# Attention and routed experts on one core: packed attention output, two banks for small products, scores by query in quarters of 64 queries, ranks in bf16

## The chip, the cores and the metric

The kernel runs as one launch on one core of a Trainium2 chip. The metric is the device time of the execution in microseconds (us). TensorE (PE) multiplies, VectorE (DVE), ScalarE (ACT) and GpSimd (POOL) do the elementwise work, SyncE (SP) issues most DMAs.

## The reference

```python
x = x + _layernorm(_L0_attn_ref(_layernorm(x), WQ, WK, WV, WO))   # 16 batches x 256 tokens x 128
x = x + _layernorm(_L0_ffn_ref(_layernorm(x), ...))
# attention: 16 heads of 8, causal softmax(Q K^T / sqrt(8)) V, then WO
# ffn: aff = x @ centroids.T; expert = argmax (8 experts); for each token its expert's
#      layernorm, w1 (128 -> 512), relu, w2 (512 -> 128), mixed with x by sigmoid(aff)
```

## The kernel before

**Tiling.** The 16 batches go through a software pipeline, one batch per step, 20 steps in all. In step i, batch i+3 is normalised and projected to Q and K, batch i+1 gets its scores by query, batch i its scores by key, exp and the product with V, and batches i-1 to i-4 the output projection, the layernorms, the choice of expert, the rank within it, and the scatter to rows sorted by expert in HBM. Afterwards 39 tiles of 128 sorted rows run through their experts.

**Q and K in three parts.** Q and K are split into three bf16 parts each (`project_qk`, `high`, `residue`, `middle`, `low`: PE, ACT, DVE, ACT, POOL). SP writes the parts to HBM (`parts_out`, L291) and reads them back in six DMAs (`parts_in`, L302 and L304) into `qaug` and `kaug`, 126 partitions deep, so that one bf16 product of depth 126 holds six products of parts.

**Scores twice.** `scores_by_query` (L802 to L812) puts queries on PSUM partitions so that DVE can take each row's maximum (`maxima`, L1082). The negated maximum, as two bf16 parts, is transposed by PE (`transpose_shift`, L787), copied by ACT (`shift_out`, L566) to `nmT`, and moved by a DMA of 8 KB (`shift`, L314, `aug<-nmT`) into the last two partitions of `qaug`: 16 source rows of each part become one long row. There are two such halves per batch, heads 0 to 7 and 8 to 15. `scores_near` and `scores_far` (L825, L834) then compute the shifted scores with keys on partitions, ACT takes exp, POOL applies the causal mask (L421, L425), and `weigh_values` (L846, L850) multiplies by V. V has 32 columns per head (8 values, a one, zeros), so four heads fill the 128 partitions of one output.

**What sets the order.** Each engine runs a stream written out by hand in its `step(i)`; semaphores join them. SP's is short: `shift(i, 1)`, `parts_out(i+2)`, `parts_in(i+2)`, `shift(i+1, 0)`, then in some steps one expert's w2. SP issues a DMA only when it has passed the waits and issues of all those ahead of it. PE's step starts with `scores_near(i, 0)`, which waits for the semaphore `sh_in[0]`, that is, until the DMA of `shift(i, 0)` has landed, and ends with `project_qk(i+3)` and one unit of scores by query.

**Scores by query before.** The work comes in 12 units of 512 columns per batch, which alternate between the two banks of `S`: 4 heads with queries 0 to 127 against keys 0 to 127, or 2 heads with queries 128 to 255 against all keys. Each begins with a product that writes the causal mask (L802, L807), and four products of 128 columns are added to it.

**Small products.** All the small products and transposes of a step (projections, transposes of x, of the output, of the maxima, the affinities and ranks) share one bank `M`. `take_m` makes PE wait before each until the one before has been read out.

Of the kernel before, what the change touches and what calls it, by code (L numbers as in the profile page):

```python
# [15 lines left out]
P = 128  # L16
# [35 lines left out]
def sandwich_kernel(nc, x, attn_w, w1x, w2t, b2, cent_t, out):  # L52
# [16 lines left out]
    CAP = (NT + 1) * P  # L69
    assert D == P and SEQ == 2 * P and B % 2 == 0  # L70

    RING = 3
# [8 lines left out]
    with ExitStack() as ctx:  # L81
# [17 lines left out]
        causal = sb("causal", [P, 4, P], BF16)  # L99
        before = sb("before", [P, P])  # L100
        ones = sb("ones", [P, P])
        mhalf = sb("mhalf", [P, NT])
# [19 lines left out]
        nmf = sb("nmf", [P, RING, NH, 2])  # L122
# [5 lines left out]
        oT = sb("oT", [P, 4, SEQ])  # L128
        rden = sb("rden", [P, 2, NH])
# [25 lines left out]
        hot = sb("hot", [P, NT, E])  # L155
        run = sb("run", [P, NT + 1, E])
# [16 lines left out]
        def carve(table, *shapes):  # L173
# [4 lines left out]
            for shape in shapes:  # L178
# [4 lines left out]
                if len(shape) == 3:  # L183
# [17 lines left out]
        O = ps("O", [P, 2, 2, SEQ])  # L201
        M = ps("M", [P, 512])

        names = ("w_attn w_cent w_ffn x_in x_next x_rest qzero kone ids_r consts pmem vmem vones "
                 "st_x agg_x ve_x rs_x nb_x xn_r xnT_r xnT_d qk_r hi_d r1_d mid_d parts_d "
# [26 lines left out]

        NA = FC // 2

        def hidden(p, c):

            if c < NA:
                return S[:, p, c * P:(c + 1) * P]
            return ST0[:, 2 * p:2 * p + 2].rearrange("p a n -> p (a n)")[:, (c - NA) * P:(c - NA + 1) * P]

# [37 lines left out]
        def _(sp):  # L278
# [110 lines left out]
        def _(pool):  # L389
# [53 lines left out]
            def scatter(b, t):  # L443

                p = b.slot(RING)
                if t == 0:
# [8 lines left out]
            g.memset(causal[:, :, :], 0.0).then_inc(s["pmem"], 1)  # L455
# [5 lines left out]
            g.affine_select(out=causal[:, :, :], in_=causal[:, :, :], compare_op=ALU.is_ge, fill=NEG, base=0,  # L461
                            pattern=[[0, 4], [-1, P]], channel_multiplier=1).then_inc(s["consts"], 1)
# [11 lines left out]
            for table, by, base in ((down, -1, E), (steps, P, 0), (slots, 1, 0), (starts, CAP, 0), (run[:, 0], CAP // P, 0)):  # L474
                g.iota(table[:, :], [[by, table.shape[-1]]], base=base, channel_multiplier=0,
                       allow_small_or_imprecise_dtypes=True).then_inc(s["consts"], 1)
            pool.wait_ge(s["ids_r"], 3)
# [60 lines left out]
        def _(act):  # L538
            a = nc.scalar

            def xnT_out(b):
# [4 lines left out]
                a.activation(xnT[:, p], M[:, 0:SEQ], ACT.Copy).then_inc(s["xnT_d"], 1)  # L546

            def high(b):
# [5 lines left out]
                a.activation(part(p, 0), M[:, :].rearrange("p (s t) -> p s t", s=2), ACT.Copy).then_inc(s["hi_d"], 1)  # L554
# [6 lines left out]
            def shift_out(b, half):  # L561
                act.wait_ge(s["shT_r"], b.times(2, half + 1))
                if b.follows(RING):
                    act.wait_ge(sh_in[half], b.times(16, 16 * (1 - RING)))
                p = b.slot(RING)
                a.activation(nmT[:, p, half], M[:, 0:P // 2].bitcast(BF16)[0:32, 0:P], ACT.Copy).then_inc(s["sh_d"], 1)  # L566

            def v_out(b):
# [20 lines left out]
            def o_out(i, half):  # L589
                act.wait_ge(s["pv"], i.times(NG, 2 * half + 2))  # L590
                if i.follows(1):
                    act.wait_ge(s["otr_r"], i.times(2))
                a.activation(oT[:, 2 * half:2 * half + 2], O[:, half], ACT.Copy).then_inc(s["o_ev"], 1)

            def onT_out(i):
# [3 lines left out]
                a.activation(onT[:, :], M[:, 0:SEQ], ACT.Copy).then_inc(s["onT_d"], 1)  # L599

            def y_out(i):
# [3 lines left out]
                a.activation(yb[:, i.slot(RING)], M[:, 0:SEQ].rearrange("p (t d) -> p t d", t=2), ACT.Copy).then_inc(s["y_d"], 1)  # L605

            def fT_out(i):
# [40 lines left out]
            def step(i):  # L648
# [5 lines left out]
                if t:  # L654
                    exp_far(t, 0)
                    shift_out(t, 1)
                if new:
                    normalise_x(new)
                if old:
                    o_out(old, 1)  # L660
# [17 lines left out]
                if t:  # L678
                    o_out(t, 0)
# [37 lines left out]
            def enter(t):  # L717
# [6 lines left out]
                a.activation(nT[:, p], (M, ST1[:, 0])[p][:, 0:P], ACT.Identity, scale=column(t, 0),  # L724
# [27 lines left out]
        def _(pe):  # L752
            mm = nc.tensor.matmul
            m_free = [[]]

            def take_m():
                for name, value in m_free[0]:
                    pe.wait_ge(s[name], value)

            def transpose_x(b):  # L760
                take_m()
                pe.wait_ge(s["xn_r"], b.times(1, 1))
                for t in (0, 1):
                    last = nc.tensor.transpose(M[:, t * P:(t + 1) * P], xn[:, b.slot(RING), t], ident[:, :])
# [3 lines left out]
            def project_qk(b):  # L768
                take_m()
                pe.wait_ge(s["xnT_d"], b.times(1, 1))  # L770
                for w in (0, 1):
                    last = mm(M[:, w * SEQ:(w + 1) * SEQ], wat[:, w], xnT[:, b.slot(RING)], start=True, stop=True)  # L772
                last.then_inc(s["qk_r"], 1)
                m_free[0] = [("hi_d", b.times(1, 1)), ("r1_d", b.times(1, 1))]

            def project_v(b):
                take_m()
# [725 lines left out]
```

## Time and profile before

| | |
|---|---|
| time, median of 3 runs | 454.77 us (454.33 to 455.31) |
| profiled execution, its own time | 454.81 us |
| its span, first to last instruction | 453.1 us |
| outside the span | 1.7 us |
| mean granted TensorE clock | 0.942 |
| PE busy | 359.6 us (79%) |
| DVE busy | 336.5 us (74%) |
| ACT busy | 250.8 us (55%) |
| POOL busy | 242.1 us (53%) |
| chain that ended last: PE, DMA, DVE, ACT | 54%, 11%, 9%, 4% |
| of it DMA `aug<-nmT` | 6% |

Busy time is the share of the span in which an engine had an instruction in flight. The chain is the sequence of work, each released by the one before, that ends with the last instruction. A row of the timeline gives start, length, engine, line, operation, output and inputs, count, and in brackets how long the engine had been idle and what ended it. The steps of the pipeline run to about 334 us, the experts' tiles after that.

### The profile page before, as it was taken

The page shows a single profiled execution, that of the slowest core. Times are in us where ns is not written, and L with a number is a line of the kernel's source. Part 1 is how long each engine was busy: PE and PEld are TensorE (multiplying, and loading weights), DVE is VectorE, ACT ScalarE, POOL GpSimd, SP SyncE. Part 2 cuts the span into 40 slices and gives each one's busy share as a digit, 9 for nine tenths or more (in the row PEclk, how much of TensorE's full clock was granted, in tenths as well). Part 3 has the DMA queues.
Part 4 walks back from the last instruction along what each step waited for, and adds up shares of the span by engine and source line. Part 5 has one row for each costly group of instructions (what it writes and reads, how often), then busy time and mean ns, then how long its engine had stood idle before and what let it go on. Part 6 is the DMA issues. An engine that isn't in the chain of part 4 may idle for free.

```text
span 453.1 us, 11940 instructions
## 1 busy us (share of the span) xinstructions
PE 359.6 (79%) x3739; PEld 286.3 (63%) x3739; DVE 336.5 (74%) x1244; ACT 250.8 (55%) x574; POOL 242.1 (53%) x334
## 2 busy tenths in 40 slices
PE   3359688979989998999899898987525798999960
PEld 1136466656767777777677766765424688888860
DVE  7748776758877887887887889575551788989880
ACT  2204457556675675675675665574203577777750
POOL 3803254534474664664664664567360266767773
PEclk9999989989999999999999999899555999999995
DMA  7661853726535535535526527021024466666720
GB/s 207 109 104 41 135 90 48 112 57 94 90 66 78 91 71 72 98 64 79 99 51 93 95 42 117 26 63 34 14 85 128 116 165 170 174 172 176 186 58 9
DMA packets 34686, 42.83 MB, mean 95 GB/s; under 512 B 5465, under 2 KB 25053, under 8 KB 33088
## 3 DMA queue, kind: packets, MB, share of 16 engines
q1 hardware_dynamic: 31744, 37.43, 42.3%
q0 software_dynamic: 2304, 4.37, 2.9%
q8 instruction: 31, 0.51, 0.6%
q14 instruction: 31, 0.25, 0.2%
q10 hardware_dynamic: 576, 0.27, 0.2%
HBM read 30.59 MB, written 11.66 MB: 93 GB/s over the span
## 4 chain that ended last, share of the span: by engine, by line
PE 54%; DMA 11%; DVE 9%; issue 9%; POOL 6%; SPq 5%; ACT 4%; POOLq 0%; DVEq 0%; ACTq 0%
PE O L846 6%; DMA aug<-nmT 6%; PE O L1006 5%; PE ST L825 5%; PE S L812 4%; PE S L993 4%; PE M L858 3%; PE M L772 3%; PE S L807 3%; PE S L805 3%; PE S L802 3%; PE O L850 3%; PE ST L993 2%; PE ST L834 2%; POOL out_x L516 2%
## 5 line engine op out<-in xcount | busy, mean ns | idle before, releaser
L1082 DVE TENSOR_REDUCE nmf<-S 128x2 f32<-128x512 f32 (+1 forms) x192 | 130.1, 680 | 53.7 <-PE S L812 26.7
L421 POOL TENSOR_SCALAR_AFFINE_SELECT p<-p 128x512 f32<-128x512 f32 x64 | 40.8, 638 | 96.9 <-ACT p L583 96.9
L583 ACT ACTIVATE p<-ST 128x1024 f32<-128x1024 f32 x64 | 65.5, 1023 | 16.6 <-PE ST L825 15.9
L812 PE MATMUL S<-aug 126*128 126x128 bf16 x512 | 51.7, 225 | 0.0
L825 PE MATMUL ST<-aug 128*128 128x256 bf16 x256 | 39.9, 279 | 14.9 <-DMA aug<-nmT 14.7
L425 POOL TENSOR_SCALAR_AFFINE_SELECT p<-p 128x512 f32<-128x512 f32 x64 | 40.9, 639 | 10.4 <-ACT p L587 7.8
L516 POOL DMA_INDIRECT out_x<-vaug,x_all x39 | 40.7, 1045 | 8.3 <-issue 6.1
L812 PEld LDWEIGHTS S<-aug 126*128 126x128 bf16 x512 | 41.2, 101 | 3.8
L526 POOL TENSOR_TENSOR rsz<-vez,mhalf 128x1 f32<-128x1 f32 x39 | 22.1, 567 | 39.0 <-DVE vez L1437 38.9
L1006 PE MATMUL O<-w_tab,vaug 128*128 x312 | 42.6, 280 | 0.0
L846 PE MATMUL O<-p,vaug 128*32 128x256 f32 x512 | 41.2, 391 | 0.3 <-POOL p L421 0.3
L451 POOL DMA_INDIRECT xs_rows<-pay,pos x32 | 32.9, 1029 | 13.1 <-DVE pos L1242 7.1
L587 ACT ACTIVATE p<-ST 128x512 f32<-128x512 f32 x64 | 38.7, 604 | 1.5 <-PE ST L834 0.3
L1006 PEld LDWEIGHTS O<-w_tab,vaug 128*128 128x128 f32 x312 | 37.8, 191 | 1.0 <-issue 0.2
L807 PE MATMUL S<-causal,identb 128*128 128x256 bf16 x128 | 36.5, 285 | 1.2 <-DVE nmf L1082 0.8
L825 PEld LDWEIGHTS ST<-aug 128*128 128x128 bf16 x256 | 23.4, 99 | 19.5 <-DMA aug<-nmT 17.1
L1408 DVE TENSOR_SCALAR vaug<-ST,w1s 128x128 f32<-128x128 f32 x78 | 23.7, 345 | 14.8 <-PE ST L993 12.8
L993 PE MATMUL S<-vaug,w1s 128*128 128x128 f32 x156 | 27.0, 297 | 7.3 <-DMA w1s<-in_w1x 3.4
L802 PE MATMUL S<-causal,identb 128*128 128x512 bf16 x64 | 26.0, 406 | 7.2 <-DMA aug<-qk_parts 7.2
L993 PEld LDWEIGHTS S<-vaug,w1s 128*128 128x128 f32 x156 | 21.2, 197 | 13.3 <-issue 6.8
L415 POOL TENSOR_TENSOR qkp<-res,qkp 128x512 bf16<-128x512 f32 x16 | 18.7, 1168 | 20.3 <-ACT qkp L559 20.3
L805 PEld LDWEIGHTS S<-aug 126*128 126x128 bf16 x256 | 21.1, 103 | 9.7 <-issue 2.2
(155 smaller groups left out, 868.4 us busy)
## 6 DMA issues: line engine op xcount, KB each, us to landing
w1s<-in_w1x SPq DMA_DIRECT2D x39, 259.0 KB
qk_parts<-qkp SPq DMA_DIRECT2D x16, 384.0 KB, 2.8
aug<-qk_parts SPq DMA_DIRECT2D x32, 192.0 KB
aug<-qk_parts SPq DMA_DIRECT2D x32, 128.0 KB
x_all<-xs_rows SPq DMA_DIRECT2D x39, 67.0 KB, 2.4
aug<-qk_parts SPq DMA_DIRECT2D x32, 64.0 KB
w_tab<-in_w2t SPq DMA_DIRECT2D x8, 256.0 KB, 5.6
out_x<-vaug,x_all POOLq DMA_INDIRECT x39
```

Source lines behind the costliest of these rows:

```text
L421: g.affine_select(out=v, in_=v, compare_op=ALU.is_ge, fill=0.0, base=0, pattern=[[0, 4], [1, P]], channel_multiplier=-1).then_inc(s["sel0" ...
L425: g.affine_select(out=v, in_=v, compare_op=ALU.is_ge, fill=0.0, base=0, pattern=[[0, 4], [1, P]], channel_multiplier=-1).then_inc(s["sel1" ...
L516: g.indirect_dma_start(out=out.rearrange("b t d -> (b t) d"), out_offset=bass.IndirectOffsetOnAxis(ap=xs[:, q, TOK:TOK + 1].bitcast(U32), ...
L583: a.activation(p0[:, gr % 2], ST0[:, :, :], ACT.Exp, scale=SCALE).then_inc(s["exp0"], 1)
L802: mm(bank, identb[:, :], causal[:, :, :], start=True, stop=False)
L807: mm(bank.rearrange("p (j c n) -> p j c n", j=2, c=2)[:, :, 1], identb[:, :], causal[:, 0:2], start=True, stop=False)
L812: last = mm(bank[:, j * SEQ + kb * P:j * SEQ + (kb + 1) * P], q[:, h, P:SEQ], k[:, h, kb * P:(kb + 1) * P], start=False, stop=(j == 1 and ...
L825: last = mm(ST0[:, j], kaug[:, p, h, 0:P], qaug[:, p, h], start=True, stop=True)
L846: mm(O[32 * j:32 * j + 32, gr // 2, gr % 2, :], vaug[:, p, 0, 4 * gr + j], p0[:, gr % 2, j], start=True, stop=False)
L993: last = mm(hidden(p, c), w1s[:, t.slot(WR), c * P:(c + 1) * P], nT[:, p], start=True, stop=True)
L1006: last = mm(O[:, p, 0, 0:D], hs[:, p, c], w2_tab[:, bass.ds(e * (FC * D) + c * D, D)], start=(c == 0), stop=(c == FC - 1))
L1082: v.tensor_reduce(dst, S[:, n % 2].rearrange("p (j n) -> p j n", j=k), op=ALU.max, axis=AX_X, negate=True).then_inc(s["red"], 1)
```

## The change

- `scores_by_query` works on quarters of 64 queries, with two heads (h and h+4) stacked on the 128 partitions, each product 64 columns wide in its weights. A quarter takes only the keys that it can see: 64, 128, 192 or 256. This makes 10 units of 512 columns per batch: in each half two of quarter 3, one of quarter 1 and two that join quarters 2 and 0. The causal mask, now 64 by 64 and doubled on the partitions, is added last.
- `maxima` takes one or two reduces per unit, 14 per batch. Since the maxima's rows now hold two heads of 64 queries, each `shift` becomes two DMAs of 4 KB.
- `weigh_values` puts the heads of an odd group 16 rows above those of the even group before it: the output takes one bank instead of two, leaves by one copy (`o_out`), four transposes and one `divide`. `v_out` takes two copies.
- The bank set free makes `M` two: `MA` and `MB`, with a list of waits each.
- The matrices of the ranks (`before`, `ones`, `hot`, `run`) are bf16, with values offset so that they are exact.
- On DVE `alphas` and `shift_parts` move by some places; on ACT `o_out` stands ahead of `normalise_x`.

```diff
+    QB = P // 2
+    UNITS = 10
-        oT = sb("oT", [P, 4, SEQ])
+        oT = sb("oT", [P, 2, SEQ])
-        O = ps("O", [P, 2, 2, SEQ])
-        M = ps("M", [P, 512])
+        O = ps("O", [P, 2, SEQ])
+        MA = ps("MA", [P, 512])
+        MB = ps("MB", [P, 512])
...
-                sp.dma_start(qaug[SHIFT:P, p, 8 * half:8 * half + 8].rearrange("c h (q t) -> c (h q) t", t=P),
-                             nmT[:, p, half]).then_inc(sh_in[half], 16)
+                for h in (0, 1):
+                    at = 8 * half + 4 * h
+                    sp.dma_start(qaug[SHIFT:P, p, at:at + 4].rearrange("c h (j t) -> c (h j) t", t=QB),
+                                 nmT[:, p, half, QB * h:QB * h + QB]).then_inc(sh_in[half], 16)
...
                 bank = S[:, n % 2]
                 q, k = qaug[0:SHIFT, p], kaug[0:SHIFT, p]
+                def score(pair, quarter, col):
+                    keys = QB * (quarter + 1)
+                    for h in (0, 1):
+                        head = 8 * half + 4 * h + pair
+                        mm(bank[QB * h:QB * h + QB, col:col + keys], q[:, head, QB * quarter:QB * quarter + QB],
+                           k[:, head, 0:keys], start=(col == 0), stop=False)
+                if kind < 2:
+                    for r in (0, 1):
+                        score(2 * kind + r, 3, 2 * P * r)
...
+                mm(masked, identb[:, :], causal[:, 0:blocks], start=False, stop=True).then_inc(s["s_r"], 1)
...
                 for j in range(4):
-                    mm(O[32 * j:32 * j + 32, gr // 2, gr % 2, :], vaug[:, p, 0, 4 * gr + j], p0[:, gr % 2, j],
-                       start=True, stop=False)
+                    mm(O[32 * j:32 * j + 32, gr // 2, :], vaug[:, p, 0, 4 * gr + j], p0[:, odd, j],
+                       start=not odd, stop=False)
...
-            def transpose_o(i, qb):
-                take_m()
-                pe.wait_ge(s["o_ev"], i.times(2, 2))
-                for gr in range(NG):
-                    last = nc.tensor.transpose(M[:, gr * P:(gr + 1) * P], oT[:, gr, qb * P:(qb + 1) * P], ident[:, :])
+            def transpose_o(i):
+                take_m(1)
+                pe.wait_ge(s["o_ev"], i.times(1, 1))
+                for qb in (0, 1):
+                    for half in (0, 1):
+                        at = 2 * qb + half
+                        last = nc.tensor.transpose(MB[:, at * P:(at + 1) * P], oT[:, half, qb * P:(qb + 1) * P], ident[:, :])
```

SP's stream in a middle step, from the second half's shift of one batch to the first half's of the next. Before:

```order
L314 DMA aug<-nmT 2x16x128 [waits st1_r,sh_d]
L291 DMA qk_parts<-qkp 128x6x256 [waits aug_in0,parts_d]
L302 DMA aug<-qk_parts 24x4096 [waits st1_r,qk_w0]
L304 DMA aug<-qk_parts 24x4096
L302 DMA aug<-qk_parts 16x4096
L304 DMA aug<-qk_parts 16x4096
L302 DMA aug<-qk_parts 8x4096
L304 DMA aug<-qk_parts 8x4096
```

The same place now:

```order
L337 DMA aug<-nmT 2x16x64 [waits st1_r,sh_d]
L337 DMA aug<-nmT 2x16x64
L312 DMA qk_parts<-qkp 128x6x256 [waits aug_in0,parts_d]
L323 DMA aug<-qk_parts 24x4096 [waits st1_r,qk_w0]
L325 DMA aug<-qk_parts 24x4096
L323 DMA aug<-qk_parts 16x4096
L325 DMA aug<-qk_parts 16x4096
L323 DMA aug<-qk_parts 8x4096
L325 DMA aug<-qk_parts 8x4096
L337 DMA aug<-nmT 2x16x64 [waits st1_r,sh_d]
L337 DMA aug<-nmT 2x16x64
```

A second DMA of the shift stands ahead of `parts_out` (L312), and another at the end.

PE's stream at the end of a step and the start of the next, where `sh_in0` is waited for. Before:

```order
L846 MATMUL O<-p,vaug 32x256 [waits sel0,o_ev]
L846 MATMUL O<-p,vaug 32x256 x3
L850 MATMUL O<-p,vaug 32x128 [waits sel1]
L850 MATMUL O<-p,vaug 32x128 x3
L772 MATMUL M<-xnT,wat 128x256 [waits xnT_d,onT_d]
L772 MATMUL M<-xnT,wat 128x256
L807 MATMUL S<-causal,identb 128x2x128 [waits red]
L812 MATMUL S<-aug 128x128 x4
L825 MATMUL ST<-aug 128x256 [waits exp0,sh_in0]
L825 MATMUL ST<-aug 128x256 x3
```

Now:

```order
L798 MATMUL MB<-xnT,wat 128x256 [waits xnT_d,v_d]
L798 MATMUL MB<-xnT,wat 128x256
L862 MATMUL ST<-aug 128x256 [waits exp0,sh_in0]
L862 MATMUL ST<-aug 128x256 x3
L835 MATMUL S<-aug 64x256 [waits red,aug_in2]
L835 MATMUL S<-aug 64x256 x3
L851 MATMUL S<-causal,identb 128x2x64
L914 MATMUL MA<-wo,onT 128x128 [waits onT_d]
L914 MATMUL MA<-wo,onT 128x128
L871 MATMUL ST<-aug 128x128 [waits exp1]
L871 MATMUL ST<-aug 128x128 x3
```

The unit between the projection (L772, now L798) and `scores_near` (L825, now L862) is gone; each unit is products of 64 weight columns with the mask behind them.

## Rows read from the trace of the kernel before

**Rows 1.** Timeline of PE at the start of three later steps and two early ones.

```profile
163.82 0.61 PE L825 MATMUL ST<-aug 128*128 128x256 bf16 x4 [1.00 <-DMA aug<-nmT]
...
180.88 0.61 PE L825 MATMUL ST<-aug 128*128 128x256 bf16 x4 [0.82 <-DMA aug<-nmT]
...
111.28 0.61 PE L825 MATMUL ST<-aug 128*128 128x256 bf16 x4 [0.71 <-DMA aug<-nmT]
129.39 0.61 PE L825 MATMUL ST<-aug 128*128 128x256 bf16 x4 [1.58 <-DMA aug<-nmT]
```

**Rows 2.** Timeline of SP's DMA issues over two steps.

```profile
149.39 0.62 SPq L314 DMA_DIRECT2D aug<-nmT  x1
150.11 0.39 SPq L291 DMA_DIRECT2D qk_parts<-qkp  x1
153.43 0.30 SPq L302 DMA_DIRECT2D aug<-qk_parts  x1
158.24 9.02 SPq L314 DMA_DIRECT2D aug<-nmT  x2
167.35 0.39 SPq L291 DMA_DIRECT2D qk_parts<-qkp  x1
170.13 0.30 SPq L302 DMA_DIRECT2D aug<-qk_parts  x1
184.59 0.39 SPq L291 DMA_DIRECT2D qk_parts<-qkp  x1
```

**Rows 3.** DMA view, 161 to 164 us: GB/s in 40 slices.

```profile
GB/s 219 0 0 0 109 0 0 0 0 0 0 3 7 3 7 7 7 7 7 10 7 3 7 7 7 10 7 3 0 0 0 0 0 0 0 0 0 0 0 0
```

**Rows 4.** DMA view, 149 to 151.5 us: busy tenths, GB/s.

```profile
DMA  0099500000000000000000009011110027999989
GB/s 0 0 480 412 206 0 0 0 0 0 0 0 0 0 0 0 0 0 0 0 0 0 0 0 262 0 25 29 41 25 12 0 49 205 303 262 311 287 254 270
```

**Rows 5.** Timeline of ACT at the start of a step.

```profile
164.18 0.63 ACT L559 ACTIVATE qkp<-res 128x512 bf16<-128x512 f32 x1 [0.97 <-DVE res L1070]
164.72 1.01 ACT L583 ACTIVATE p<-ST 128x1024 f32<-128x1024 f32 x1
165.62 0.38 ACT L605 ACTIVATE yb<-M 128x256 f32<-128x256 f32 x1
166.36 0.25 ACT L566 ACTIVATE nmT<-M 32x128 bf16<-32x128 bf16 x1
```

**Rows 6.** Timeline of POOL: the last part of Q and K.

```profile
165.97 1.18 POOL L415 TENSOR_TENSOR qkp<-res,qkp 128x512 bf16<-128x512 f32 x1
```

**Rows 7.** Waits, 60 to 300 us: who for whom, total, times, longest.

```profile
PE ST L825 <- DMA aug<-nmT: 11.6, 10, 3.1
...
PE M L764 <- DVE on L1109: 4.2, 12, 0.5
PE M L787 <- ACT yb L605: 3.8, 8, 0.6
```

**Rows 8.** Timeline of PE inside steps.

```profile
160.25 0.39 PE L812 MATMUL S<-aug 126*128 126x128 bf16 x4
160.57 0.64 PE L846 MATMUL O<-p,vaug 128*32 128x256 f32 x8
161.02 0.40 PE L850 MATMUL O<-p,vaug 128*32 128x128 f32 x8
...
168.12 0.39 PE L805 MATMUL S<-aug 126*128 126x128 bf16 x4
168.35 0.61 PE L858 MATMUL M<-ident,oT 128*128 128x128 f32 x4
168.79 0.39 PE L834 MATMUL ST<-aug 128*128 128x128 bf16 x4
```

**Rows 9.** Groups by line, whole span.

```profile
L1082 DVE TENSOR_REDUCE nmf<-S 128x2 f32<-128x512 f32 (+1 forms) x192 | 130.1, 680 | 53.7 <-PE S L812 26.7
L805 PEld LDWEIGHTS S<-aug 126*128 126x128 bf16 x256 | 21.1, 103 | 9.7 <-issue 2.2
```

More of the change, by code:

```diff
@@ L239, in hidden, with unit, units @@
             return ST0[:, 2 * p:2 * p + 2].rearrange("p a n -> p (a n)")[:, (c - NA) * P:(c - NA + 1) * P]
+        def unit(gr, u):
+            return 5 * (gr // 2) + 3 * (gr % 2) + u
+        def units(gr):
+            return 2 if gr % 2 else 3
         def iterations(eng, step):
@@ L473, in _ @@
             g.iota(fill_at[:, :], [[0, 1]], base=E * CAP, channel_multiplier=1).then_inc(s["ids_r"], 1)
-            for table, by, base in ((down, -1, E), (steps, P, 0), (slots, 1, 0), (starts, CAP, 0), (run[:, 0], CAP // P, 0)):
+            for table, by, base in ((down, -1, E), (steps, P, 0), (slots, 1, 0), (starts, CAP, -BASE), (run0, CAP // P, -P)):
                 g.iota(table[:, :], [[by, table.shape[-1]]], base=base, channel_multiplier=0,
                        allow_small_or_imprecise_dtypes=True).then_inc(s["consts"], 1)
+            pool.wait_ge(s["consts"], 11)
+            for table, by in ((run[:, 0], run0), (beforeb, before), (onesb, ones)):
+                g.tensor_copy(table[:, :], by[:, :]).then_inc(s["consts"], 1)
             pool.wait_ge(s["ids_r"], 3)
@@ L918, in _ @@
             pe.wait_ge(s["consts"], 6)
+            pe.wait_ge(s["mask_d"], 2)
             for gr in range(NG):
-                for u in range(3):
+                for u in range(units(gr)):
                     scores_by_query(Nth(0), gr, u)
@@ L970, in _ @@
             iterations(pe, step)
-            take_m()
-            mm(M[:, 0:E], ones[:, :], run[:, NT], start=True, stop=True).then_inc(s["total_r"], 1)
+            take_m(0)
+            mm(MA[:, 0:E], onesb[:, :], run[:, NT], start=True, stop=True).then_inc(s["total_r"], 1)
             pe.wait_ge(s["rt"], 1)
@@ L1078, in maxima @@
[L1078 to L1083 removed]
+                if u >= units(gr):
+                    return
+                p, n = b.slot(RING), unit(gr, u)
+                half, kind = n // 5, n % 5
@@ new lines, in maxima, with most @@
+                dve.wait_ge(s["s_r"], b.times(UNITS, n + 1))
+                def most(quarter, first, count, src):
+                    return v.tensor_reduce(nmf[:, p, half, first:first + count, quarter], src, op=ALU.max, axis=AX_X,
+                                           negate=True)
+                if kind == 2:
+                    last = most(1, 0, 4, S[:, n % 2].rearrange("p (r n) -> p r n", r=4))
+                else:
+                    two = S[:, n % 2].rearrange("p (r n) -> p r n", r=2)
+                    if kind < 2:
+                        last = most(3, 2 * kind, 2, two)
+                    else:
+                        most(2, 2 * (kind - 3), 2, two[:, :, 0:3 * QB])
+                        last = most(0, 2 * (kind - 3), 2, two[:, :, 3 * QB:4 * QB])
@@ L1085, in maxima_and_stats @@
+                last.then_inc(s["red"], 1)
             def maxima_and_stats(i, b, gr, u):
                 maxima(b, gr, u)
-                if i.k < 2:
-                    x_stats(i.k + 3, 3 * gr + u)
+                if i.k < 2 and u < units(gr):
+                    x_stats(i.k + 3, unit(gr, u))
             def shift_parts(b, half):
                 p = b.slot(RING)
-                src = nmf[:, p, 8 * half:8 * half + 8].rearrange("p h q -> p (h q)")
-                dve.wait_ge(s["red"], b.times(12, 6 * half + 6))
+                src = nmf[:, p, half].rearrange("p r j -> p (r j)")
@@ L1095, in shift_parts @@
+                dve.wait_ge(s["red"], b.times(UNITS, 5 * half + 5))
                 if b.follows(RING):
```

244 lines of the change are left out of this document (123 added, 121 removed).

## The prediction

> **What bounds the kernel now.** I read the table of the profile first: PE is busy 79% of the span and DVE 74%, so PE looks like the bound. Then I read the timeline of PE over a few steps for the places where it stands still. At the start of nearly every step it does: the first product of `scores_near` starts at 163.82 and 180.88 after 1.00 and 0.82 us of idling, both put down to the DMA `aug<-nmT` [rows 1]. Over 60 to 300 us PE lost 11.6 us there, more than to any bank [rows 7]. The next question is what makes this 8 KB late, so I read SP's issues. One step of it: shift issued at 149.39, taking 0.62; `parts_out` at 150.11; the first `parts_in` at 153.43; the next batch's first shift at 158.24; the next `parts_out` at 167.35 and then 184.59, so a step takes 17.24 us [rows 2]. The DMA view shows why the shift issued at 158.24 lands so late. In the idle queue of 149 to 151.5 us the small packets (5 slices of 0.0625 us at 12 to 41 GB/s) begin about 1.2 us after the issue at 149.39 and take 0.3 us [rows 2, 4]. The shift of 158.24 shows its small packets only from about 161.8 to 163.1, behind the last large ones of `parts_in` at 161.3 [rows 3]. So it waits in the queue for `parts_in`, and its own issue time is hidden.
>
> This closes a circle of one step: `scores_near` starts (163.82); ACT takes exp_near (164.72), the y copy (165.62), exp_far and `shift_out` (166.36) [rows 5]; SP issues `shift(i, 1)`, 0.62 us, which must have begun by 166.63 and ends just ahead of `parts_out` at 167.35 [rows 2]; `parts_in` follows 2.8 us later at 170.13, its data flows, the queued shift goes, and `scores_near` starts at 180.88. The other input of `parts_out`, the `low` part on POOL, ends at 165.97 + 1.18 = 167.15, so it is ready at about the same time [rows 6]. A second circle is almost as long: in ACT's stream exp_near at 164.72 follows `middle` (164.18), which waited for DVE's `residue` [rows 5]. `scores_near` has its four products issued by about 164.4, so the DMA circle has a slack of at most 0.3 us against the second one. I take 0.3: the DMA circle alone needs 16.95 us in later steps. In early ones, whose w2 loads share the queue, it has no slack: 129.39 - 111.28 = 18.1 us from one start to the next, with a wait of 1.58 [rows 1].
>
> **The change part by part.**
>
> *Shift as two DMAs.* The second half's shift stands ahead of `parts_out` on SP. Its second DMA has as many rows (2x16) of half the length, and I cost its issue like the first: 0.62 us plus 0.04 between two issues, 0.66 us on the circle. Bounds: 0.3, the shortest issue in SP's rows (`parts_in`), and 0.62 + 0.1 [rows 2]. In the first half's shift the second issue is hidden behind the data of `parts_in` (3.3 us of queue), but its packets are not: 8 KB took 0.3 us in an idle queue and 1.2 us behind `parts_in` [rows 3, 4]. With twice as many packets of half the size the addition is between 0 (both DMAs side by side) and 1.2; I take 0.45, nearest to the idle row. The sum for the circle is 16.95 + 0.66 + 0.45 = 18.06 us, or 0.83 more than 17.24 in a later step and 1.11 more in an early one.
>
> The DMA view shows one busy tenth while the shift's packets go [rows 4], that is, few of the 16 engines. By the Trainium skill, "DMA: Bandwidth & Descriptors", section "Why a DMA increments its semaphore by 16 and not by 1", a DMA uses the largest number of engines that divides the outermost dimensions of both sides, here 2 and 32, thus 2. By that rule the two DMAs, if they get the same two engines, queue behind one another, and the sum would lie above mine.
>
> *The two banks.* They free PE of the wait for y before the transposed shift (3.8 us in all) and of the wait for `on` before the transpose of x (4.2 us) [rows 7]. `residue` no longer stands behind a reduce, since the unit after `project_qk` is gone. All this shortens the second circle and PE's work between two DMA waits; on the first circle it shortens nothing, for ACT's chain from `scores_near` to `shift_out` remains: exp, y, exp, copy. What is late next is the same DMA, and PE waits for it longer. I cost these gains at nothing. If the DMA's cover were gone, they would be worth 0.3 + 0.35 us a step.
>
> *Scores by query on PE.* Before, a batch has 12 x 512 columns of products and 4096 of masks, 10,240 in all. Four products of 128 columns take 0.23 us [rows 8], so 10,240 columns, or 80 times 128, take 80 x 0.057 = 4.6 us. Now it is 10,240 columns of products and 2048 of masks. The four heads of `weigh_values` (eight passes of 256 columns in 161.02 - 160.57 = 0.45 us, where one after another at that rate they would take 0.9) show that products in different column groups run side by side. If the two stacked heads do so too, it is 5120 + 2048 columns = 3.2 us; if not, 5.5. To that come changes between narrow and full products. `L812` takes 0.32 us ahead of the narrow `L846` where `L805` takes 0.23 ahead of full ones [rows 8]: 0.09 each, 20 of them per step, 1.8 us. So PE's units go from 4.6 to 5.0 or 7.3 us.
>
> A rule speaks against the change here: the Trainium skill, "TensorEngine Tiling (Array Packing)", section "Tiling Modes", says that changing the tiling mode drains TensorE. The 0.09 us above is such a drain in this trace, and by it each of the ten units pays for two. The same page's promise of up to twice the speed for 64 columns would save 2.3 us of 5.5 and lose 1.8 of it to the drains.
>
> *The other PE work.* Four transposes less, at 168.79 - 168.35 = 0.44 us for four [rows 8], and about 0.35 us less for the ranks as one bf16 pass each: -0.8 us. PE's work per step, now 17.24 less waits of about 1.6, or 15.6, becomes 15.2 (15.6 + 5.0 - 4.6 - 0.8) or 17.5 (with 7.3). Both fit under 18.06, so its net cost is nothing. Above, if no weight load of the 64 is hidden at 0.10 us each [rows 9], units cost 6.4 + 1.8 + 0.9 = 9.1 us and PE's work 19.3.
>
> *DVE, ACT, POOL.* A reduce of 512 columns takes 0.68 us; 12 become 14 over 5120 columns instead of 6144 [rows 9], so DVE saves between 0.4 and 1.0 us a step, plus one pair of division. It idled before nearly each reduce, waiting for PE, so this is hidden. ACT saves one output copy and gains one V copy, off the circle.
>
> *Start and end.* The first batch's units run alone, ten instead of twelve, at half clock: -0.7 us, from 0 to -1.5. The last steps have no `parts_in`; they are chains of small products, and one set of four transposes, its division and two rank passes go from some of them: -1.7 us, from 0 to -2.5. The expert tiles are unchanged.
>
> *The sum.* `parts_out` inside a step occurs 14 times (of 16; two are at the start). The 5 early starts cost 1.11 each, the 9 later ones 0.83: 5.6 + 7.5 = 13.0. One early `parts_out` was held by `low` and not by the shift: -0.6. 13.0 - 0.6 - 2.4 = +10.0 us. The profiled execution took 454.81 us, 0.04 above the median of the runs, so the same sum holds for both: 464.8, say 465 us.
>
> **Rivals.**
>
> *The DMA's additions are small or hidden, and the banks pay (faster).* If the second issue overlaps the first, and its packets go beside the others, the DMA circle stays at 16.95 us and the second circle, now shorter by the y copy and the reduce, no longer holds it: 9 x 0.3 + 2.4 = 5 us less, 450. If moreover the wait at `scores_near` is shorter than the trace has it (a shift that goes ahead of the last packets of `parts_in`), PE's 15.2 us plus rest waits of 0.8 decide: 14 x 1.2 + 2.4, or 19 us less, 436. For it: the banks' waits are real [rows 7], and the idle queue moves 8 KB in 0.3 us. Against it: the 0.62 us stand bare between shift and `parts_out` in each step. It decides once the two additions are under 0.3 us a step.
>
> *They cancel.* Additions of 0.3 to 0.5 us, as with the lower issue price: 14 x 0.2 - 2.4, about 0: 453.9 to 455.7.
>
> *PE takes over (slower still).* At 19.3 us a step the circle of DMA is covered: 14 x 2.06 - 2.4 = +26, 481 us. For it: 64 loads per step, and the drains. Against it: the narrow fp32 loads of `weigh_values` are hidden.
>
> **How the numbers follow.** Forecast (DMA circle longer): 0.62, with its own range 458 (additions of 0.66 a step without the packets) to 474 (0.66 + 0.9). Faster: 0.21. Cancel: 0.07. PE takes over: 0.10. A measurement of this kernel can tell 0.2%, 0.9 us, from no change. Slower 0.72, same 0.07, faster 0.21. The range for 8 in 10 reaches from 446 (most of the faster cases) to 474.
>
> **What would show it.** Right: SP's rows have two `aug<-nmT` issues of about 0.6 us ahead of `parts_out`, steps of about 18.1 us from one `parts_out` to the next, PE idle 1.5 to 3 us before `scores_near`, and no wait for `y` or `on` at the small products. PE busy per unit about 0.5 us. Wrong: steps under 17.2 us, or PE not idle before `scores_near`, or an issue well under 0.6 us.

## The result, and the profile after

| | before | changed |
|---|---|---|
| time, median of the runs side by side (4 each) | 454.55 us (452.79 to 455.31) | 466.17 us (465.51 to 467.83) |
| profiled execution, its own time | 454.81 us | 465.54 us |
| its span | 453.1 us | 463.6 us |
| mean granted TensorE clock | 0.942 | 0.914 |
| PE, DVE busy | 359.6, 336.5 us | 354.5, 312.9 us |
| chain that ended last: PE, DMA | 54%, 11% | 42%, 25% |

The changed kernel takes 1.0244 times as long (95% interval 1.0204 to 1.0284). The forecast was 465 us, slower, by a longer circle of DMA. Ratios and differences of kernels go by runs within 1.5% of the fastest of their kernel; a_warm, below, had three slower ones in ten, and its other seven have a median of 455.1 us. PE and DVE have less work than before, and the chain has moved from PE to the DMA `aug<-nmT`. The page of the changed kernel, its clock, its chain and three groups (busy, mean ns, idle time ahead and its releaser):

```profile
PEclk9999997989999899899999998799755999999995
...
PE 42%; DMA 25%; SPq 10%; issue 7%; DVE 7%; POOL 5%; ACT 2%; POOLq 0%; DVEq 0%; ACTq 0%
DMA aug<-nmT 19%; PE S L835 9%; PE O L883 5%; PE ST L862 5%; PE S L851 5%; DMA w1s<-in_w1x 3%; PE ST L871 2%; SPq L337 2%; PE O L887 2%; PE MA L914 2%; PE S L1031 2%; SPq L386 2%; SPq L390 2%; POOL out_x L542 2%; PE ST L1031 1%
...
L1126 DVE TENSOR_REDUCE nmf<-S 128x2 f32<-128x512 f32 (+3 forms) x224 | 113.5, 531 | 70.7 <-PE S L851 68.8
L835 PE MATMUL S<-aug 126*64 126x256 bf16 (+3 forms) x1024 | 71.5, 254 | 2.8 <-DMA aug<-qk_parts 1.6
L862 PE MATMUL ST<-aug 128*128 128x256 bf16 x256 | 39.5, 278 | 38.0 <-DMA aug<-nmT 38.0
```

Waits of 60 to 300 us; the columns are those of [rows 7]. There PE waited 11.6 us for the shift, and now 33.1. The waits for y and for `on` ahead of the small products are gone:

```profile
PE ST L862 <- DMA aug<-nmT: 33.1, 13, 4.1
```

SP's issues in three steps. Line 337 is the shift, 312 `parts_out`, 323 the first `parts_in` (314, 291 and 302 in [rows 2]); a row with x4 spans both halves' pairs and the time between them:

```profile
162.36 9.62 SPq L337 DMA_DIRECT2D aug<-nmT  x4
172.08 0.39 SPq L312 DMA_DIRECT2D qk_parts<-qkp  x1
174.84 0.30 SPq L323 DMA_DIRECT2D aug<-qk_parts  x1
...
189.32 1.26 SPq L337 DMA_DIRECT2D aug<-nmT  x2
190.69 0.39 SPq L312 DMA_DIRECT2D qk_parts<-qkp  x1
194.75 0.30 SPq L323 DMA_DIRECT2D aug<-qk_parts  x1
...
226.86 1.26 SPq L337 DMA_DIRECT2D aug<-nmT  x2
228.22 0.39 SPq L312 DMA_DIRECT2D qk_parts<-qkp  x1
230.99 0.31 SPq L323 DMA_DIRECT2D aug<-qk_parts  x1
```

The pair takes 1.26 us where one took 0.62 [rows 2]. From the start of `scores_near` to `parts_out` it is 228.22 - 224.03 = 4.19 us in the last of these steps, and was 167.35 - 163.82 = 3.53 [rows 1, 2]: 0.66 more. The starts of `scores_near` on PE (compare [rows 1]), and further rows of the same timeline, which answer to [rows 8]:

```profile
150.18 0.61 PE L862 MATMUL ST<-aug 128*128 128x256 bf16 x4 [2.14 <-DMA aug<-nmT]
167.87 0.61 PE L862 MATMUL ST<-aug 128*128 128x256 bf16 x4 [1.00 <-DMA aug<-nmT]
185.29 0.61 PE L862 MATMUL ST<-aug 128*128 128x256 bf16 x4 [2.16 <-DMA aug<-nmT]
205.59 0.61 PE L862 MATMUL ST<-aug 128*128 128x256 bf16 x4 [3.58 <-DMA aug<-nmT]
224.03 0.61 PE L862 MATMUL ST<-aug 128*128 128x256 bf16 x4 [1.71 <-DMA aug<-nmT]
224.57 0.41 PE L835 MATMUL S<-aug 126*64 126x256 bf16 x4
224.91 0.23 PE L851 MATMUL S<-causal,identb 128*128 128x128 bf16 x1
224.98 0.66 PE L914 MATMUL MA<-wo,onT 128*128 128x128 f32 x4
...
241.34 0.61 PE L862 MATMUL ST<-aug 128*128 128x256 bf16 x4 [2.05 <-DMA aug<-nmT]
...
277.32 0.61 PE L862 MATMUL ST<-aug 128*128 128x256 bf16 x4 [2.79 <-DMA aug<-nmT]
```

From 150.18 to 277.32 are seven steps, 18.16 us each; 18.06 was forecast for a later step. But they are not alike. Busy time and granted clock of an early step and of five of the seven, and then one microsecond at a time near the start of the longest:

```profile
core 0: us, PE busy (x) PEld busy (x) DVE busy (x) ACT busy (x) POOL busy (x), PEclk, DMA share, GB/s
74.13:93.04 18.91, 17.02 (x192) 10.65 (x193) 11.55 (x36) 10.62 (x20) 9.30 (x13) 0.84 0.47 79
167.87:185.29 17.42, 15.26 (x201) 10.09 (x201) 13.50 (x54) 11.55 (x25) 11.22 (x16) 1.00 0.47 80
185.29:205.59 20.30, 16.72 (x201) 10.92 (x201) 12.57 (x49) 11.39 (x24) 11.71 (x17) 0.92 0.42 71
205.59:224.03 18.44, 16.74 (x200) 10.98 (x201) 12.29 (x48) 11.07 (x24) 8.49 (x13) 0.91 0.42 70
224.03:241.34 17.31, 15.26 (x200) 10.10 (x201) 12.84 (x51) 11.58 (x25) 10.60 (x15) 1.00 0.47 79
241.34:259.27 17.93, 15.27 (x201) 10.10 (x201) 12.56 (x49) 11.26 (x24) 10.93 (x16) 1.00 0.45 76
...
186.00:187.00 1.00, 1.00 (x8) 0.69 (x5) 0.36 (x1) 0.96 (x1) 1.00 (x1) 0.50 0.21 69
187.00:188.00 1.00, 1.00 (x9) 0.74 (x10) 0.33 (x1) 0.38 (x1) 0.68 (x2) 0.50 0.00 0
188.00:189.00 1.00, 1.00 (x10) 0.46 (x14) 0.19 (x1) 0.60 (x1) 0.31 (x1) 0.50 0.00 0
189.00:190.00 1.00, 1.00 (x18) 0.58 (x10) 0.89 (x3) 0.29 (x2) 0.33 (x1) 0.81 0.00 0
```

The four of the seven at full clock take 17.31 to 18.05 us, 17.7 in the mean. In the other three PE is granted 0.50, which is 1.2 of 2.4 GHz, for some 3 us after it stood at the DMA (2.14 us ahead of 150.18, 2.16 ahead of 185.29, 3.58 ahead of 205.59), just when it has the products that ACT's chain to the shift needs; four early steps have 0.84 to 0.92 in the mean. At 241.34 it stood 2.05 us and at 259.27 it stood 2.66, and kept its clock, so the wait alone doesn't tell when the clock falls. Of the 13 steps from 55.30 to 296.27 the clock fell in 8. In the 5 others it is 4.19 to 4.21 us from `scores_near` to `parts_out`, in the 8 it is 4.28 to 5.91. In the step from 185.29, `parts_out` comes 190.69 - 185.29 = 5.40 us after `scores_near`, 1.2 more than at 224.03. The same step has its first `parts_in` 4.06 us after `parts_out` instead of 2.8, as the step from 93.04 has it 4.49 after. No run explains this, and it comes in other kernels too (4.0 to 4.5 us in two steps each of a_warm and b_split1).

### The profile page after: what moved, and what is told of

It reads as the page before. It is cut to its first block, busy times and chain, and to the rows that moved or that the text cites. A ratio compares the mean times of both kernels' runs of the same rounds, so it can differ in the third digit from the quotient of the medians.

```text
span 463.6 us, 12161 instructions
## 1 busy us (share of the span) xinstructions
PE 354.5 (76%) x3866; PEld 252.3 (54%) x3866; DVE 312.9 (68%) x1249; ACT 248.1 (54%) x574; POOL 244.8 (53%) x337
## 4 chain that ended last, share of the span: by engine, by line
PE 42%; DMA 25%; SPq 10%; issue 7%; DVE 7%; POOL 5%; ACT 2%; POOLq 0%; DVEq 0%; ACTq 0%
DMA aug<-nmT 19%; PE S L835 9%; PE O L883 5%; PE ST L862 5%; PE S L851 5%; DMA w1s<-in_w1x 3%; PE ST L871 2%; SPq L337 2%; PE O L887 2%; PE MA L914 2%; PE S L1031 2%; SPq L386 2%; SPq L390 2%; POOL out_x L542 2%; PE ST L1031 1%
## 5 line engine op out<-in xcount | busy, mean ns | idle before, releaser
L1126 DVE TENSOR_REDUCE nmf<-S 128x2 f32<-128x512 f32 (+3 forms) x224 | 113.5, 531 | 70.7 <-PE S L851 68.8
L444 POOL TENSOR_SCALAR_AFFINE_SELECT p<-p 128x512 f32<-128x512 f32 x64 | 40.8, 638 | 104.8 <-ACT p L611 104.8
L835 PE MATMUL S<-aug 126*64 126x256 bf16 (+3 forms) x1024 | 71.5, 254 | 2.8 <-DMA aug<-qk_parts 1.6
L862 PE MATMUL ST<-aug 128*128 128x256 bf16 x256 | 39.5, 278 | 38.0 <-DMA aug<-nmT 38.0
L835 PEld LDWEIGHTS S<-aug 126*64 126x64 bf16 x1024 | 35.1, 113 | 30.4 <-issue 21.7
L862 PEld LDWEIGHTS ST<-aug 128*128 128x128 bf16 x256 | 23.7, 99 | 46.8 <-DMA aug<-nmT 43.7
L448 POOL TENSOR_SCALAR_AFFINE_SELECT p<-p 128x512 f32<-128x512 f32 x64 | 42.2, 659 | 11.6 <-ACT p L615 8.3
L883 PE MATMUL O<-p,vaug 128*32 128x256 f32 x512 | 44.8, 420 | 0.7 <-POOL p L444 0.7
L851 PE MATMUL S<-causal,identb 128*128 128x256 bf16 (+1 forms) x160 | 43.5, 272 | 0.0
L474 POOL DMA_INDIRECT xs_rows<-pay,pos x32 | 33.1, 1034 | 13.2 <-DVE pos L1296 7.4
L1464 DVE TENSOR_SCALAR vaug<-ST,w1s 128x128 f32<-128x128 f32 x78 | 23.6, 344 | 14.9 <-PE ST L1031 13.5
L851 PEld LDWEIGHTS S<-causal,identb 128*128 128x128 bf16 x160 | 15.5, 97 | 25.2 <-issue 16.9
L887 PE MATMUL O<-p,vaug 128*32 128x128 f32 x512 | 27.2, 283 | 0.0
L871 PE MATMUL ST<-aug 128*128 128x128 bf16 x256 | 26.7, 231 | 0.0
L731 ACT ACTIVATE vaug<-x_all 128x128 f32<-128x128 f32 x39 | 19.3, 494 | 13.5 <-DMA x_all<-xs_rows 13.5
```

The lines of the kernel that those rows point to most:

```text
L444: g.affine_select(out=v, in_=v, compare_op=ALU.is_ge, fill=0.0, base=0, pattern=[[0, 4], [1, P]], channel_multiplier=-1).then_inc(s["sel0" ...
L448: g.affine_select(out=v, in_=v, compare_op=ALU.is_ge, fill=0.0, base=0, pattern=[[0, 4], [1, P]], channel_multiplier=-1).then_inc(s["sel1" ...
L835: mm(bank[QB * h:QB * h + QB, col:col + keys], q[:, head, QB * quarter:QB * quarter + QB], k[:, head, 0:keys], start=(col == 0), stop=False)
L851: mm(masked, identb[:, :], causal[:, 0:blocks], start=False, stop=True).then_inc(s["s_r"], 1)
L862: last = mm(ST0[:, j], kaug[:, p, h, 0:P], qaug[:, p, h], start=True, stop=True)
L883: mm(O[32 * j:32 * j + 32, gr // 2, :], vaug[:, p, 0, 4 * gr + j], p0[:, odd, j], start=not odd, stop=False)
```

## Experiments

Each ran in a group with the kernel before, whose medians were 454.85 us in the first group (the first four below), 454.43 in the second (the next four), and 454.96 in the third. The ratios are the recorded ones, taken against these runs; they are not quotients of the medians and differ from them by up to 0.4% (a_early has 0.9697, and 442.82 / 454.85 is 0.9736).

### The double shift alone, in the kernel before

**b_split1**: the second half's shift, ahead of `parts_out`, as two DMAs. **b_split0** the same for the first half only, **b_split01** for both.

```diff
-                sp.dma_start(qaug[SHIFT:P, p, 8 * half:8 * half + 8]..., nmT[:, p, half]).then_inc(sh_in[half], 16)
+                parts = 2 if half in (1,) else 1
+                n = P // parts
+                for k in range(parts):
+                    sp.dma_start(dst[:, :, n * k:n * k + n], nmT[:, p, half, n * k:n * k + n]).then_inc(sh_in[half], 16)
```

> The kernel before, with the second half's shift (the one ahead of parts_out on SP) sent as two DMAs of 4 KB; nothing else is changed. Theory (the DMA circle): 0.66 us more issue ahead of parts_out, less the slack of 0.3 us: +0.36 us in 9 later steps and +0.66 in 5 early ones, +6.5 us, about 461 us; steps of about 17.6 us from parts_out to parts_out. Rival (the loss of the changed kernel is PE's work on narrow products, not the DMA): no change, 454.6 us.

> The kernel before, with only the first half's shift (the one queued behind parts_in) sent as two DMAs of 4 KB. Theory: its issue is hidden behind the data of parts_in, its packets are not: +0.45 us, less the slack of 0.3: 9 x 0.15 + 5 x 0.45 = +3.6 us, about 458 us. If the packets go side by side: no change. Rival (PE's work is the loss): no change, 454.6 us.

> The kernel before, with both halves' shifts as two DMAs of 4 KB each, as the changed kernel has them, and none of its other parts. Theory: the whole loss is here and somewhat more, since the gains at the start and the end (2.4 us) are missing: 5 x 1.11 + 9 x 0.81 = +12.8, about 467.5 us. Rival (PE's work is the loss): 454.6 us. Mixed: in between.

Measured: 465.91 us (ratio 1.0246, interval 1.0193 to 1.0298), 457.24 (1.0035, 1.0011 to 1.0058) and 467.12 (1.0235, 1.0201 to 1.0269). So 4 KB pieces ahead of `parts_out` cost the kernel before as much as the whole change costs, and the same split behind `parts_in` costs about a fifth of that, inside what was expected for it. The first was 5 us above what was expected. Three of its steps (columns as above) show the surplus, which is not spread over the steps:

```profile
167.89:185.17 17.28, 15.61 (x190) 12.38 (x193) 13.87 (x50) 11.35 (x24) 10.14 (x15) 1.00 0.47 79
203.30:221.25 17.95, 17.16 (x191) 13.30 (x193) 11.95 (x44) 11.31 (x23) 8.64 (x13) 0.90 0.44 72
259.39:278.01 18.62, 17.16 (x190) 13.50 (x193) 12.77 (x45) 11.11 (x23) 8.00 (x12) 0.91 0.42 69
```

The first, at full clock, takes 17.28, hardly more than before. In the others the clock fell, and PE was busy 1.5 us more with the same instructions. That is not all of the surplus. The step before the third, 239.88 to 259.39, takes 19.51 us at full clock, with its first `parts_in` 4.50 us after `parts_out` instead of 2.8, and the one before the second, 185.17 to 203.30, takes 18.13 at full clock. How much of the 11 us is the clock's was not tried in this kernel.

### The shift behind `parts_out`

**a_early** is the changed kernel, **b_early** the one before, with this edit of SP's order:

```diff
-                if b := at(i, 0):
-                    shift(b, 1)
                 if b := at(i, 2):
                     parts_out(b)
+                if b := at(i, 0):
+                    shift(b, 1)
```

> The changed kernel, with parts_out(i+2) ahead of shift(i, 1) in SP's stream, so that the two issues of the shift fall into the time in which SP waits for the parts to be written. Theory: parts_out then goes as soon as POOL's low part is done. From the rows of before and after: scores_near to scores_far of group 3 12.5 us, to the end of low 7.2, parts_out 0.2, to scores_near 14.1: 34.0 us for two steps, 17.0 instead of 18.1: 14 x 1.1 = 15 us less than the changed kernel, about 451 us, or a little below the kernel before. Rival (PE's work sets the step): 466 us as the changed kernel.

> The kernel before, with only SP's order changed: parts_out(i+2) ahead of shift(i, 1). Theory: in later steps nothing is won, since ACT's middle and y copy behind DVE's residue hold the step at 17.24 us whatever the DMA does; the early steps win up to 1 us each: about 451 us. The gain of the same edit on the changed kernel (442.8) then needs the two banks. Rival (the order of SP alone makes it, the rest of the change is worth nothing): about 443 us here too.

Measured: 442.82 us (0.9697, 0.9663 to 0.9731) and 450.82 (0.9882, 0.9812 to 0.9951). With the shift out of the way the changed kernel is 23 us faster than it was and 12 us faster than the one before. SP's rows of a_early, one pair of steps:

```profile
173.85 0.38 SPq L312 DMA_DIRECT2D qk_parts<-qkp  x1
175.86 1.27 SPq L337 DMA_DIRECT2D aug<-nmT  x2
177.23 0.38 SPq L323 DMA_DIRECT2D aug<-qk_parts  x1
...
192.45 0.38 SPq L312 DMA_DIRECT2D qk_parts<-qkp  x1
192.93 1.27 SPq L337 DMA_DIRECT2D aug<-nmT  x2
195.22 0.30 SPq L323 DMA_DIRECT2D aug<-qk_parts  x1
```

`parts_out` no longer follows the shift. The steps now come in pairs, 18.60 (173.85 to 192.45) and 15.47 us (192.45 to 207.92), 34.1 for two, which was expected at 34.0; the miss of 8 us to the fast side is mostly in the early steps: five of them take 122.77 - 39.52 = 83.3 us where the changed kernel takes 95.1, 11.9 less, and I had given them 5.5. That is the largest single proof for the circle: nothing but the order of two issues differs. With it PE is busy 31.3 of the 34.1 us of this pair, so little but PE's own work is left there.

b_early came out as expected: its late steps stay at 17.24 us. Where its 4 us lie is open, for its profiled run was the slowest of the four (453.80 us). So the same order is worth 4 us in the kernel before and 23 in the changed one, and under this order the rest of the change is worth 450.82 - 442.82 = 8 us.

### The first half's shift on ACT's queue

The prediction says that this shift "waits in the queue for `parts_in`". If so, a queue of its own should set it free. **b_act0** does it to the kernel before, **a_act0** to the changed one, **a_early_act0** together with the edit above. SP's `shift(b, 0)` goes, and `shift_out` on ACT ends with:

```diff
+                if half == 0:
+                    act.wait_ge(s["sh_d"], b.times(2, 1))
+                    ...
+                    for h in (0, 1):
+                        act.dma_start(qaug[SHIFT:P, p, 4 * h:4 * h + 4]..., nmT[:, p, 0, QB * h:QB * h + QB]).then_inc(sh_in[0], 16)
```

> The kernel before, with the first half's shift issued by ACT, on its own queue, right after it has written nmT, so that it isn't queued behind parts_in. Theory: PE doesn't wait for aug<-nmT at the start of a step any more, but the later steps stay at 17.24 us, held by residue, middle, exp and the y copy; about 1 us off each of 5 early steps: about 450 us. Rival (the DMA circle alone holds the kernel before): 14 steps at about 16 us, about 437 us.

> The changed kernel, with the first half's two shifts issued by ACT on its own queue. SP's order is as in the changed kernel. Theory: the circle now runs over scores by query, which wait for parts_in itself (aug_in) 0.5 us after the start of a step, and is shorter by the shift's packets and landing, some 1.6 us: steps of about 16.5 us, about 444 us. Rival (only the issue ahead of parts_out counts): 466 us less little.

> The changed kernel with both: parts_out ahead of shift(i, 1) on SP, and the first half's shifts on ACT's queue. Theory: no circle of DMA is left that is longer than PE's work, about 15.3 us and some small waits: steps of about 16.0 us against 17.05 of the one edit alone: about 432 us, below both kernels. Rival (PE's narrow products are the bound after all): no gain over 442.8.

Measured: 459.81 us (1.0115, 1.008 to 1.015), 469.97 (1.031, 1.024 to 1.038) and 449.82 (0.9864, 0.9783 to 0.9945). All three missed, by 10, 26 and 18 us. The timeline of a_act0 in one step, ACT and then PE, and below it the DMA view of 186 to 190 us (GB/s in 40 slices):

```profile
182.65 0.27 ACT L587 ACTIVATE nmT<-MA 32x128 bf16<-32x128 bf16 x1 [0.75 <-PE MA L815]
182.95 1.27 ACTq L593 DMA_DIRECT2D aug<-nmT  x2
...
189.99 0.61 PE L864 MATMUL ST<-aug 128*128 128x256 bf16 x4 [2.54 <-DMA aug<-nmT]
```

```profile
GB/s 0 82 0 0 82 82 82 164 0 82 82 82 0 82 164 0 0 0 0 164 0 0 4 9 13 15 21 19 1 257 343 43 0 0 0 0 0 43 0 0
```

The shift is issued at once, at 182.95, and lands 7.0 us later all the same. The small packets (4 to 21 GB/s) run at about 188.2 to 188.8 us, after the large ones of `parts_in`, whose last issue was at 181.11. So SP's order is not what holds this shift. The packets of another queue wait just as long while `parts_in` has the DMA engines. The Trainium skill, "DMA: Bandwidth & Descriptors", section "Issuing engines are not separate DMA queues", warns of just this; the 7.0 us agree with it. In b_act0 the late steps stay at 17.24 us, and `scores_near` starts 13.2 to 13.7 us after `parts_out`, as before (13.53 in [rows 1, 2]).

ACT now spends 1.27 us a step on issues, but this is not what made a_act0 slower: its steps at full clock take 17.2 to 17.9 us and have 4.20 or 4.21 from `scores_near` to `parts_out`, as in the changed kernel (4.19). In the others it is up to 6.11, with granted clocks of 0.84 to 0.92, and the mean clock is 0.899 against 0.914. Why the clock falls more often here, and why a_early_act0 lost 7 us against a_early, is open.

### The parts of the change apart

**o_scores** is the changed kernel with the scores by query, their maxima and mask, and the single shift of before; packing, two banks and the bf16 ranks stay. In its shift:

```diff
-                for h in (0, 1):
-                    at = 8 * half + 4 * h
-                    sp.dma_start(qaug[SHIFT:P, p, at:at + 4]..., nmT[:, p, half, QB * h:QB * h + QB]).then_inc(sh_in[half], 16)
+                sp.dma_start(qaug[SHIFT:P, p, 8 * half:8 * half + 8]..., nmT[:, p, half]).then_inc(sh_in[half], 16)
```

**o_scores_early** has the order of a_early as well.

> The changed kernel with the scores by query, their mask, the maxima and the single shift DMA per half put back as they were before; the packed output, the two banks and the bf16 ranks stay. Theory (the loss is the doubled shift, the other parts are worth little while the DMA circle holds): 9 x 0.25 + 1.7 = 4 us less than the kernel before, about 450.5 us. Rival (something in the packing or the banks costs, too): above 455 us.

> The same, and parts_out ahead of shift(i, 1) on SP. Against the changed kernel with that order (442.8 us), whose later steps took 17.04 us on average, the two-step circle loses the 0.45 us of packets: 16.8 us a step, 14 x 0.24 = 3.4 us less, about 440 us. Rival (the quarters of 64 queries are worth something once the circle is opened, by DVE's 10 units or PE's work): above 443 us.

Measured: 448.42 us (0.9876, 0.9836 to 0.9915) and 442.61 (0.974, 0.9679 to 0.98). Both within 3 us of what was expected. SP's rows of o_scores:

```profile
178.91 0.62 SPq L334 DMA_DIRECT2D aug<-nmT  x1
179.65 0.39 SPq L311 DMA_DIRECT2D qk_parts<-qkp  x1
182.47 0.30 SPq L322 DMA_DIRECT2D aug<-qk_parts  x1
...
196.21 0.39 SPq L311 DMA_DIRECT2D qk_parts<-qkp  x1
```

A step takes 16.56 us here, and 16.5 in the mean of the late ones, while PE still stands about 1.5 us ahead of `scores_near`: this is the DMA circle without the second issue. I had it at 16.95. Banks, packing and bf16 ranks are thus worth 6.5 us by themselves, and the scores by 64 queries with their double shift cost 466.17 - 448.42 = 18 us. Once the shift is out of the circle they cost nothing that these runs can tell: a_early and o_scores_early differ by 0.2 us.

### PE kept busy at the wait

**a_warm** puts 16 products of the identity, whose result is overwritten, ahead of the wait for the shift; they are extra work. **a_early_warm** has the order of a_early too.

```diff
-                if gr % 2 == 0:
-                    pe.wait_ge(sh_in[gr // 2], i.times(32, 32))
                 if i.k > 0 or gr > 0:
                     pe.wait_ge(s["exp0"], i.times(NG, gr))
+                if gr == 0:
+                    for j in range(16):
+                        mm(ST0[:, j % 4, 0:P], identb[:, :], identb[:, :], start=True, stop=True)
+                if gr % 2 == 0:
+                    pe.wait_ge(sh_in[gr // 2], i.times(32, 32))
```

> The changed kernel, with 16 products of 128 columns by the identity put ahead of PE's wait for sh_in[0] at the start of a step; they are overwritten. In the profile of the changed kernel 4 of the last 9 steps with a DMA wait of 2 us or more have TensorE at its lower clock for some 3 us after it, and those steps took 17.7 to 20.3 us against 17.3 to 18.05. Theory (part of the loss is the clock, which falls when PE stands idle at that wait): the granted clock rises from 0.91 towards 0.94 and about 4 us go: 462 us. Rival (the clock's fall is hidden like PE's other work): 466 us or, with 0.9 us of products in 14 steps not hidden, up to 470.

> The same products in the changed kernel with parts_out ahead of shift(i, 1) (442.8 us without them). There every other step waits about 2 us for the shift and the others hardly at all. Theory of the clock: 1 to 2 us won in 4 long steps, 0.9 us lost in the 7 steps without a wait unless these only shorten the next wait: about 441 us, from 438 to 446. Rival: 443 us or more.

Measured: 456.9 us (1.0, 0.9958 to 1.0042; 452.96 to 465.87 in ten runs) and 438.06 (0.963, 0.9597 to 0.9663). Steps of a_warm, columns as above:

```profile
55.97:75.54 19.57, 17.39 (x207) 11.06 (x207) 12.05 (x44) 10.48 (x19) 7.45 (x11) 0.86 0.50 84
92.17:109.71 17.54, 16.10 (x215) 11.02 (x215) 12.32 (x44) 11.16 (x23) 8.15 (x13) 1.00 0.53 86
199.26:216.87 17.61, 16.15 (x216) 11.07 (x217) 12.57 (x49) 11.25 (x24) 10.24 (x15) 1.00 0.47 79
```

PE does more and the kernel takes 11 us less than the changed one (466.17 - 455.1), measured in different groups. The clock falls in only 2 of the 13 steps from 55.97 to 289, in the first shown (0.86) and in the one from 146.38 (0.90), where in the changed kernel it fell in 8 of 13. The gain is 7 us more than I had expected. With the clock up, `parts_out` comes 4.19 to 4.48 us after `scores_near`; summed over the 13 steps, what goes beyond 4.19 is 2.4 us here and 8.1 in the changed kernel. These 5.7 us are most of the 7.3 by which the two profiled executions differ (465.54 and 458.25). `scores_near` still waits 1.3 to 1.6 us for the DMA in most steps, so the circle is the same as in the changed kernel, without the fall: four steps in a row, from one `parts_out` at 185.75 to that at 256.24, take 17.6 us each. The spread of the ten runs is wide, and only in part the clock's: 460.13 and 461.53 us were granted 0.938 and 0.937, and 458.25 only 0.930. The Trainium skill, "TensorE: Matmul & The Clock Gate", section "HAM oscillation — how this bites in real kernels", says that idle gaps of PE let its clock fall. The trace agrees in part: it fell after gaps of 2.16 and 3.58 us and not after one of 2.66. a_early_warm is the fastest of all kernels here, 3.7% under the one before.

## Why the prediction was right

**Where the time lies.** Taken by `parts_out` on SP, third to last: 42.23 to 270.79 before, 41.85 to 282.59 after.

| stretch | forecast | measured |
|---|---|---|
| ahead of the third `parts_out` | -0.7 | -0.4 |
| five early steps | +5.0 | +4.6 |
| later ones (nine forecast, eight between these two `parts_out`) | +7.5 | +7.6 |
| behind the last | -1.7 | -1.3 |
| sum | +10.0 | +10.5 (span) |

**The second issue**: 0.66 forecast and 0.66 measured (4.19 against 3.53). b_split1 puts nearly the whole slowdown on it and b_split0 a fifth of that on the other half, as the prediction had it: one is on the circle, the other beside `parts_in`. a_early, which takes it off, turns the result round.

**The slack** was mis-sized. "I take 0.3: the DMA circle alone needs 16.95": o_scores runs that circle in 16.5, so 0.75 of each step was slack, and the whole second issue fell into it. What this takes away is 0.45 us a step. "At most 0.3" was read at one place, ACT's start on exp, and not from the whole circle; in the kernel before its two parts take as little as 3.33 and 12.96 us, 16.3 together.

**The packets** were given 0.45. From `parts_out` to the next `scores_near` o_scores needs 13.0 us in the mean of eight late steps (12.24 to 13.42). With the pairs it is 13.1 to 13.2 in five steps of the changed kernel and 13.3 to 13.5 in five of a_warm, so they cost 0.2 to 0.4. From `scores_near` to `parts_out` o_scores mostly needs 3.4, which would make the second issue 0.8. Together this is the forecast's 1.1 us all the same: at full clock the step is 4.19 + 13.4 = 17.6 us, as a_warm has it, that is, 16.5 + 1.1 and not 18.06. No run here shows whether the two DMAs share their engines.

**The clock** was missing. With PE standing 2 to 4 us at the DMA, its clock falls in part of the steps, and the fall delays the very chain that feeds the next shift. a_warm, which still has two such falls, sizes it at 11 us for the whole kernel, 0.8 a step. In the seven late steps it is less: 18.16 - 17.6 = 0.56, of which 0.39 is the later `parts_out` of three steps and 0.18 the late `parts_in` of one. So the time came out right by luck: a slack too small by 0.45 stood in for a clock that was left out. The cause, the circle with the second issue, holds.

**Why the shift is late** was half wrong. It does wait for `parts_in`, but not through SP's queue: b_act0 and a_act0 gave it another and it landed no sooner. For the forecast it made no difference.

**PE's units** were given 5.0 to 7.3 us. The trace of the changed kernel: `L862` takes 224.57 - 224.03 = 0.54 ahead of the narrow products, where the same four (`L825`) took 0.44 to 0.45 ahead of a full one in the kernel before, so the drain is 0.10. Four passes of 256 take 0.34 from start to the next start, and the mask 0.07 ahead of `L914`. Unit by unit this is 0.51 to 0.57, ten of them 5.5 us. The stacked heads do run side by side and no load shows. PE's work in the step from 224.03 is 17.31 less the wait of 2.05 at its end, 15.26 us, which is its busy time (15.2 forecast), so "PE takes over" was wrong.

**The banks** were costed at nothing while the DMA's cover holds. In the changed kernel nothing speaks against it, though no run took the banks out of it. With the single shift, in o_scores, they are worth 6.5 us together with the packing.

**The rivals.** "Faster" needed additions under 0.3 us a step and "cancel" 0.3 to 0.5. At full clock the step grew by 17.6 - 17.24 = 0.36 us, so without the clock's fall "cancel" would have been the outcome, and a_warm, at 1.0 times before, bears this out. I gave it 0.07, too little for a slack read from one row.

**Two slips of the sum.** 18.06 - 17.24 is 0.82 and not 0.83. The upper end, 474, is 14 x 1.56 - 2.4 and leaves out the slack of 0.3 and the 0.6 that the main sum takes off; with them it is 471.

## What to carry to other kernels

Before splitting a DMA, find what the issuing engine does behind it: the second issue of the same size of pattern costs as much as the first, and in front of the transfer that closes a circle it cost more here than all the work that the change saved. If a circle is bound by DMA, first move what need not be ahead of the closing transfer, and only then save work on the engines; here the order of two lines was worth 23 us in the changed kernel and 4 in the one before. When a wait on TensorE grows, count also what its clock does after the wait.

## What the runs showed of the hardware

- A DMA of 2x16 rows of 256 bytes takes SP 0.62 us to issue, and a pair with rows of 128 bytes takes 1.26, so halving the rows saved nothing.
- A transfer on another engine's queue finds the DMA engines just as full: 7.0 us for 8 KB behind `parts_in`.
- Sixteen useless products ahead of a wait kept the clock at 1.00 in 11 of 13 steps, where it had been 5, and the time fell by 11 us.
- The small DVE operation `eneg<-eneg,pay` (128x2) took 14.0 us in 16 before and takes 2.5 in 16 in the changed kernel, where it stands elsewhere in DVE's order. The cause was not tried. It is off the path that sets the end.

```profile
L1217 DVE SCALAR_TENSOR_TENSOR eneg<-eneg,pay 128x2 f32<-128x2 f32 x16 | 14.0, 873 | 0.9 <-ACT eneg L624 0.9
L1271 DVE SCALAR_TENSOR_TENSOR eneg<-eneg,pay 128x2 f32<-128x2 f32 x16 | 2.5, 153 | 0.0
```
